# Exponentials over two PSUM banks, with root, turned tokens and logits rearranged, in an attention and mixture-of-experts kernel

## The chip, the cores and the metric
One core of a Trainium2 chip runs the whole program. A core has TensorE (matrix products, with separate weight loads), VectorE, ScalarE, GpSimd (called POOL) and SyncE (SP, whose queue issues most DMAs). They run side by side and wait for one another by semaphores. The metric is the device time of one execution, in microseconds (us).

## The reference
A block on 8 sequences of 1024 tokens with 256 features, in float32:

```python
x = x + attention(layernorm(x))      # 16 heads of 16, softmax(q k^T / 4) v, rotary turn on the last 256 tokens
x = x + ffn(layernorm(x))
# ffn: scores = softmax(h @ gate_w.T); each of 16 experts takes its top 128 tokens of a sequence,
#      eo = (gelu(x_tok @ Wg.T) * (x_tok @ Wu.T)) @ Wd.T * score, added back to its tokens;
#      a shared expert of the same shape (256 -> 512 -> 256) runs on all tokens.
# layernorm: (x - mean) / sqrt(var + 1e-5)
```
The input has 8 x 1024 rows.

## The kernel before, in words
Three stages follow each other: attention, the shared expert, the 16 experts.

**Attention.** The work of a sequence ("batch" b) is 64 steps, S = 0 to 63, and V = 64 b + S counts over all 512. Eight steps are a unit: four heads and half the queries. In step V, TensorE computes for four heads a score tile of 128 keys x 512 queries with the keys on the partitions ("turned scores", L811, two before and two after the weighing), ScalarE takes the exponential of each (L646), and two steps later (LAG) TensorE multiplies them with the values (`weigh_values`, L822, "the weighing"), accumulating eight steps in one PSUM bank `pv`. The softmax needs each query's maximum before that, so 12 steps ahead (LEAD) TensorE computes the same scores with the queries on the partitions (L800) into a ring of three banks, and VectorE takes four maxima a step out of it (L515). POOL splits the maxima of a unit into three bfloat16 parts (`split_maxima`), and SP turns them into the query tiles by a DMA transpose (`turn_maxima`).

The order is written by hand. `ORDER` lists everything that passes through the four banks `rot`: the four exponentials ("ex", V, j), then the items that `beside(V)` gives. The table BESIDE places these at a step: q, k and v of the next sequence, "xt" (its transposed tokens), and of the sequence before "aot", "proj", "x2t" and the gate's logits "lg"; "ot" (a finished unit) comes in steps S % 8 == 3. `PLACE` gives an item's number n: it uses bank n % 4. TensorE fills a bank when ScalarE has emptied item n - 4:

```python
        pe.wait_ge(rot_done, n - ROT + 1)          # L729
```
All engines keep their own program order. TensorE's in a step is: score rows m, m+1 (each waits for its ring bank, L798), turned scores 0 and 1, the weighing of V-2, score rows m+2, m+3, turned scores 2 and 3, the items beside. ScalarE's is: exponentials 0 to 3, in steps V % 8 == 1 the copy of `pv` (`evacuate`, L696) after exponential 2, then the items. The first weighing of the next unit, in a step S % 8 == 2, waits for that copy (L819).

VectorE takes four maxima a step, and in some steps joins the maxima of a unit (L521), takes reciprocals (L527), layernorm statistics (`gather_stats`, S = 0 to 3 and 21 to 24; `merge_stats`), and 1/sqrt(var + eps) by an integer trick and three Newton steps (`newton`, `rsqrt_step`, L36 to L50, S = 7 to 12 and 26 to 31, one operation at a time between maxima). POOL applies the layernorm (`normalise`, S = 13 to 16 and 33 to 36). "x2t" copies leave the second layernorm's transposed tokens in `XT`, which the next sequence's "aot" overwrites. `shift_logits` and `finish_gates` are the gate's softmax.

**Shared expert.** 16 chunks of 512 tokens. TensorE turns a chunk's tokens (`turn_tokens`, L1296, eight transposes) between products of the chunk before; ScalarE and VectorE split them into a high and a low part; `up` and `down` are the products in three passes (`three`, L61 to L63). The tokens come from the DRAM tensor `xn2` that attention has stored (`store_xn2`).

**Experts.** 32 chunks of 512 gathered rows run through the same function, with transposes of their own, and their results are added by indirect DMAs.

Of the kernel before, what the change touches and what calls it, by code (L numbers as in the profile page):

```python
# [65 lines left out]
def attention(nc, d, ident, SC, B):  # L66
# [36 lines left out]
    def beside(V):  # L103
# [7 lines left out]
        if S in table:  # L111
# [9 lines left out]
            + [("proj", B - 1, i) for i in range(TT)] + [("x2t", B - 1, h, half) for half in range(2) for h in range(KH)]  # L121
            + [("lg", B - 1, half) for half in range(2)])

# [15 lines left out]
    with ctx:  # L139
# [43 lines left out]
        nt1 = sb("nt1", [P, TT], F32)  # L183
        nt2 = sb("nt2", [P, TT], F32)
        shifted = sb("shifted", [P, TT, E], F32)
        powers = sb("powers", [P, TT, E], F32)
# [6 lines left out]
        ring = [ctx.enter_context(nc.psum_tensor(f"ring{i}", [P, 512], F32)) for i in range(RING)]  # L193
        rot = [ctx.enter_context(nc.psum_tensor(f"rot{i}", [P, 512], F32)) for i in range(ROT)]
        pv_bank = ctx.enter_context(nc.psum_tensor("pv", [P, 512], F32))
# [6 lines left out]
        x1_out = sem("x1_out")  # L202
        xn2_out = sem("xn2_out")
        wh_ready = sem("wh_ready")
        wl_ready = sem("wl_ready")
# [3 lines left out]
        bo_ready = sem("bo_ready")  # L209
        rstd_ready = [sem(f"rstd_ready{n}") for n in range(2)]  # L210
        xn_ready = [sem(f"xn_ready{h}") for h in range(2)]
        xn2_ready = [sem(f"xn2_ready{h}") for h in range(2)]
# [27 lines left out]
        def _(sp):  # L240
# [24 lines left out]
            def store_xn2(b):  # L265
                for h in range(2):
                    sp.wait_ge(xn2_ready[h], 2 * (b + 1))
                sp.dma_start(rows("xn2", b), XN2[:]).then_inc(xn2_out, 16)

            def turn_heads(b, g):  # L270

                sp.wait_ge(rope_done, 2 * ROPE_TILES * (b + 1))
                sp.wait_ge(q_biased, TT * (b + 1))
                sp.wait_ge(rot_done, done(("k", b, 5)))
                if b:
                    sp.wait_ge(rot_full, done(("ex", STEPS * (b - 1) + 16 * g + 15, 3)))
# [17 lines left out]
            for b in range(B):  # L294
# [22 lines left out]
                if b < B - 1:  # L317
                    turn_maxima(n + 8)
            store_x1(B - 1)
            store_xn2(B - 1)  # L320
            sp.wait_ge(x1_out, 16 * B)
            sp.wait_ge(xn2_out, 16 * B)

        @block.gpsimd
        def _(pool):
            own = Tally(pool_own)
            for n in range(2):
# [69 lines left out]
            def add_bias(b, n):  # L397
# [3 lines left out]
                nc.gpsimd.tensor_tensor(x, x, b_o[:].unsqueeze(1).to_broadcast([P, 2, H]), ALU.add).then_inc(bias_ready, 1)  # L401

            def normalise(n, b, out, src, ready, quarter):

                pool.wait_ge(rstd_ready[n], b)
                i = slice(2 * quarter, 2 * quarter + 2)
                shape = [P, 2, H]
                own.inc(nc.gpsimd.tensor_tensor(out[:, i, :], src[:, i, :], mv[n][:, i, 0:1].to_broadcast(shape),
                                                ALU.subtract))
                own.wait(pool)  # L410
                nc.gpsimd.tensor_tensor(out[:, i, :], out[:, i, :], rstd[n][:, i].unsqueeze(2).to_broadcast(shape),
                                        ALU.mult).then_inc(ready[quarter // 2], 1)
# [24 lines left out]
            for V in range(LAST):  # L437
# [15 lines left out]
                if more and b and S == 10:  # L453
                    clear_maxima(b + 1)
                if more and 13 <= S <= 16:
                    normalise(0, b + 2, XA, XA, xn_ready, S - 13)
# [9 lines left out]
        def _(dve):  # L466
# [10 lines left out]

            def merge_stats(n, tiles):

                own.wait(dve)  # L480
                for i in tiles:
                    own.inc(nc.vector.bn_aggr(mv[n][:, i, :], stats[:, i, :]))

# [45 lines left out]
            def shift_logits(b):  # L529

                dve.wait_ge(rot_done, done(("lg", b, 1)))
                own.inc(nc.vector.reduce_max(top[:], LG[:], AX.X))
# [34 lines left out]
            for V in range(-LEAD, LAST):  # L567
# [6 lines left out]
                if V >= 13 and V % 8 == 5:  # L574
                    weighted((V - 13) // 8)
                if more and 7 <= S <= 12:
                    newton(0, 2 * (S - 7))
                if prev and 26 <= S <= 31:
                    newton(1, 2 * (S - 26))
                if m < CHECKS:  # L580
# [11 lines left out]
                if more and S in (4, 5):  # L592
                    merge_stats(0, range(4 * (S - 4), 4 * (S - 3)))
                if more and 7 <= S <= 12:
                    newton(0, 2 * (S - 7) + 1)
                if prev and 21 <= S <= 24:
                    dve.wait_ge(x1_ready, TT * (b - 1) + 2 * (S - 20))
                    gather_stats(XR, (2 * (S - 21), 2 * (S - 21) + 1))
                if prev and S == 25:
                    for h in range(2):  # L600
                        dve.wait_ge(xn2_ready[h], 2 * (b - 1))
                    merge_stats(1, range(TT))
                if prev and 26 <= S <= 31:
                    newton(1, 2 * (S - 26) + 1)
                if prev and S == 50:
                    shift_logits(b - 1)
                if prev and S == 53:
                    finish_gates(b - 1)
# [23 lines left out]
        def _(act):  # L632
# [3 lines left out]
            def empty(item):  # L636
# [5 lines left out]
                if kind == "ex":  # L642
                    _, V, j = item
                    if j == 0 and V >= P_STEPS:
                        act.wait_ge(pv_done, V - P_STEPS + 1)
                    out = nc.scalar.activation(PR[V % P_STEPS][:, j, :], R[:], ACT.Exp, scale=0.25)  # L646
                elif kind in ("xt", "aot", "x2t"):
                    _, b, h, half = item
                    if kind == "xt" and b >= 2:
                        act.wait_ge(as_ready, 4 * (b - 1))  # L650
# [35 lines left out]
                elif kind == "lg":  # L686
                    _, b, half = item
                    if b:
                        act.wait_ge(shifted_ready, b)
                    out = nc.scalar.copy(LG[:, 4 * half:4 * half + 4, :], R[:, 0:4 * E].rearrange("p (t e) -> p t e", e=E))  # L690
                out.then_inc(rot_done, 1)

            def evacuate(unit):
# [28 lines left out]
        def _(pe):  # L722
# [15 lines left out]
            def fill(item):  # L738
# [38 lines left out]
                elif kind == "lg":  # L777
                    _, b, half = item
# [77 lines left out]
def feed_forward(nc, d, ident, SC, WT, IX, W, WH, WL, shared_out, B, shared):  # L856
# [20 lines left out]
    with ctx:  # L877
# [5 lines left out]

        XG = [sb(f"XG{c}", [P, CT, D], F32) for c in range(2)]
        XH = [sb(f"XH{c}", [P, KD, N], FR) for c in range(2)]
# [87 lines left out]
        def _(sp):  # L973
            if shared:
# [126 lines left out]
        def _(act):  # L1101
# [54 lines left out]
        def _(dve):  # L1156
# [131 lines left out]
        def _(pe):  # L1288
# [46 lines left out]

            turn_tokens(0, 0)
            if shared:
# [4 lines left out]
            def group(r, first, last):  # L1342
                for k in range(K):
# [20 lines left out]

def program(nc, d, B):
    with ExitStack() as ctx:
        SC = ctx.enter_context(nc.sbuf_tensor("gate_scores", [P, 1024 // P, B * E], F32))
# [40 lines left out]
```

## Time and profile before
| what | value |
|---|---|
| time, median of 3 runs | 2406.83 us (2402.03 to 2407.79) |
| the profiled execution's own time | 2401.16 us |
| its span | 2399.3 us |
| busy share: PE, DVE, ACT, POOL | 92%, 78%, 65%, 37% |
| granted TensorE clock, mean | 0.976 |

The busy share of each engine over the span in 40 slices of 60 us (9 is 90% or more) shows the stages: attention to slice 25, the shared expert to about slice 30, then the experts.

```profile
PE   4899999999999999999999987899997999999996
DVE  4999999999999999999999994566663554555553
ACT  2499888898888898898898886333332343434332
POOL 4051362451451451542542230000004666666664
```
A row of the page is one group of instructions: line, engine, operation, output and input tiles, count, then the busy time and the mean duration in ns. A busy TensorE is not one at its peak, since matrix products overlap.

### The profile page before, as it was taken

The page shows a single profiled execution, that of the slowest core. Times are in us where ns is not written, and L with a number is a line of the kernel's source. Part 1 is how long each engine was busy: PE and PEld are TensorE (multiplying, and loading weights), DVE is VectorE, ACT ScalarE, POOL GpSimd, SP SyncE. Part 2 cuts the span into 40 slices and gives each one's busy share as a digit, 9 for nine tenths or more (in the row PEclk, how much of TensorE's full clock was granted, in tenths as well). Part 3 has the DMA queues.
Part 4 walks back from the last instruction along what each step waited for, and adds up shares of the span by engine and source line. Part 5 has one row for each costly group of instructions (what it writes and reads, how often), then busy time and mean ns, then how long its engine had stood idle before and what let it go on. Part 6 is the DMA issues. An engine that isn't in the chain of part 4 may idle for free. (4 is left out here: it accounts for less than half of the span.)

```text
span 2399.3 us, 42479 instructions
## 1 busy us (share of the span) xinstructions
PE 2218.2 (92%) x15630; PEld 1288.6 (54%) x15630; DVE 1883.3 (78%) x3505; ACT 1561.1 (65%) x3040; POOL 895.3 (37%) x1287
## 2 busy tenths in 40 slices
PE   4899999999999999999999987899997999999996
PEld 3233333333333333333343323788886888888886
DVE  4999999999999999999999994566663554555553
ACT  2499888898888898898898886333332343434332
POOL 4051362451451451542542230000004666666664
PEclk8799999999999999999999999899998999999998
DMA  4002013012022121111112111323223455454543
GB/s 112 5 25 34 17 41 69 17 48 62 16 62 50 29 63 34 34 58 34 34 43 32 34 43 38 132 87 97 79 71 104 90 112 115 87 111 109 108 94 36
DMA packets 206756, 147.81 MB, mean 62 GB/s; under 512 B 109952, under 2 KB 193792, under 8 KB 206592
## 3 DMA queue, kind: packets, MB, share of 16 engines
q1 hardware_dynamic: 182016, 112.08, 17.3%
q0 software_dynamic: 24576, 33.57, 8.1%
q8 instruction: 100, 1.64, 0.3%
q14 instruction: 64, 0.52, 0.1%
HBM read 78.50 MB, written 41.94 MB: 50 GB/s over the span
## 5 line engine op out<-in xcount | busy, mean ns | idle before, releaser
L515 DVE TENSOR_REDUCE sb_MX<-ring 128x1 f32<-128x512 f32 x2048 | 1281.9, 680 | 67.7 <-PE ring L800 51.5
L646 ACT ACTIVATE sb_PR<-rot 128x512 f32<-128x512 f32 x2048 | 1119.5, 608 | 145.7 <-PE rot L811 130.2
L800 PE MATMUL ring<-sb_KT,sb_QT 32*128 32x512 bf16 x2048 | 526.6, 391 | 92.3 <-DVE sb_MX L515 76.9
L822 PE MATMUL pv<-sb_PR,sb_VA 128*32 128x512 f32 x4096 | 546.5, 606 | 2.6 <-ACT sb_OT L696 0.6
L800 PEld LDWEIGHTS ring<-sb_KT,sb_QT 32*128 32x128 bf16 x2048 | 129.9, 91 | 707.4 <-DVE sb_MX L515 649.0
L811 PE MATMUL rot<-sb_QT,sb_KT 32*128 32x512 bf16 x2048 | 405.1, 386 | 0.9
L1113 ACT ACTIVATE ex_GL<-ex_gu 128x512 f32<-128x512 f32 x128 | 76.5, 597 | 348.6 <-PE ex_gu L63 346.4
L1180 DVE TENSOR_TENSOR ex_HF<-ex_GL,ex_gu 128x512 f32<-128x512 f32 x128 | 87.4, 682 | 252.0 <-ACT ex_GL L1113 252.0
L1077 POOL DMA_INDIRECT out<-ex_YS,ex_rows_out x128 | 208.9, 1632 | 44.1 <-issue 43.7
L1034 POOL TENSOR_TENSOR ex_pool_scratch<-identity 128x1 f32<-128x1 f32 x96 | 35.1, 366 | 472.4 <-POOLq L877 325.8
L61 PE MATMUL ex_gu<-ex_XH,weights_high 128*128 128x512 f32 x512 | 201.1, 393 | 2.4 <-DVE ex_XL L1172 2.4
L62 PE MATMUL ex_gu<-ex_XL,weights_high 128*128 128x512 f32 x512 | 200.7, 392 | 0.0
L63 PE MATMUL ex_gu<-ex_XH,weights_low 128*128 128x512 f32 x512 | 200.5, 392 | 0.0
L364 POOL CAST sb_QP<-sb_MX 128x16 bf16<-128x16 f32 x64 | 16.3, 255 | 421.2 <-DVE sb_MX L521 421.2
L1113 ACT ACTIVATE sh_GL<-sh_gu 128x512 f32<-128x512 f32 x64 | 38.2, 597 | 175.9 <-PE sh_gu L63 175.9
L61 PE MATMUL ex_y<-weights_high,ex_HH 128*128 128x256 f32 x512 | 148.2, 289 | 2.9 <-DVE ex_HL L1184 2.9
L822 PEld LDWEIGHTS pv<-sb_PR,sb_VA 128*32 128x32 f32 x4096 | 80.9, 108 | 123.2 <-issue 65.2
L63 PE MATMUL ex_y<-weights_high,ex_HL 128*128 128x256 f32 x512 | 145.7, 285 | 0.0
L62 PE MATMUL ex_y<-weights_low,ex_HH 128*128 128x256 f32 x512 | 145.7, 285 | 0.0
L61 PE MATMUL rot<-sb_WH,sb_XH 128*128 128x256 f32 x384 | 129.5, 337 | 14.6 <-ACT sb_PR L646 5.7
L1055 POOL DMA_INDIRECT ex_XG<-xn,ex_rows_in x128 | 125.7, 982 | 40.3 <-issue 39.6
L1180 DVE TENSOR_TENSOR sh_HF<-sh_GL,sh_gu 128x512 f32<-128x512 f32 x64 | 43.6, 682 | 103.3 <-ACT sh_GL L1113 103.2
(158 smaller groups left out, 4042.8 us busy)
## 6 DMA issues: line engine op xcount, KB each, us to landing
sb_XA<-x SPq DMA_DIRECT2D x8, 1024.0 KB, 5.7
sb_XR<-x SPq DMA_DIRECT2D x8, 1024.0 KB, 5.7
out<-sb_XR SPq DMA_DIRECT2D x8, 1024.0 KB, 4.6
xn<-sb_XN SPq DMA_DIRECT2D x8, 1024.0 KB, 4.4
sh_XG<-xn SPq DMA_DIRECT2D x16, 512.0 KB, 5.9
sh_X<-out SPq DMA_DIRECT2D x16, 512.0 KB, 5.2
weights<-WgT SPq DMA_DIRECT2D x16, 512.0 KB, 4.0
weights<-WuT SPq DMA_DIRECT2D x16, 512.0 KB, 6.4
```

Source lines behind the costliest of these rows:

```text
L61: nc.tensor.matmul(out, a_hi, b_hi, start=first, stop=False)
L62: nc.tensor.matmul(out, a_hi, b_lo, start=False, stop=False)
L63: return nc.tensor.matmul(out, a_lo, b_hi, start=False, stop=last)
L515: nc.vector.reduce_max(MX[:, unit % 2, half, j, qt % 4:qt % 4 + 1], ring[m % RING][:], AX.X).then_inc(ring_done, 1)
L646: out = nc.scalar.activation(PR[V % P_STEPS][:, j, :], R[:], ACT.Exp, scale=0.25)
L800: nc.tensor.matmul(ring[m % RING][:], QT[g][r, P * qt:P * qt + P], KT[g][r, 512 * half:512 * half + 512], start=True, stop=True, tile_posi ...
L811: nc.tensor.matmul(R[:], KT[g][r, P * kt:P * kt + P], QT[g][r, 512 * qh:512 * qh + 512], start=True, stop=True, tile_position=(r.start, 0) ...
L822: out = nc.tensor.matmul(pv_bank[head(j), :], VA[b % 2][:, kt, 4 * g + j, :], PR[V % P_STEPS][:, j, :], start=(kt == 0), stop=(kt == TT - 1))
L1055: nc.gpsimd.indirect_dma_start(out=XG[k % 2][:, t, :], out_offset=None, in_=d["xn2"], in_offset=bass.IndirectOffsetOnAxis(ap=rows_in[:, b: ...
L1077: nc.gpsimd.indirect_dma_start(out=d["out"], out_offset=bass.IndirectOffsetOnAxis(ap=rows_out[:, b:b + 1], axis=0), in_=YS[k % 2][:, t, :] ...
L1113: nc.scalar.activation(GL[f % 2][:], gu[f % 2][:, 0, 0:N], ACT.Gelu).then_inc(gelu_ready, 1)
L1180: nc.vector.tensor_tensor(HF[f % 2][:], GL[f % 2][:], gu[f % 2][:, 1, 0:N], ALU.mult).then_inc(hf_ready, 1)
```

## The change
- **Exponentials.** The four `rot` banks become one tensor. A new function takes the exponential of banks n and n+1 in one instruction of 128 x 1024 and releases both at its end, except where n % 4 == 3 (the two don't lie next to each other). The copy of `pv` stands after exponential 3.
- **Root.** `newton` leaves VectorE's loop. At S = 7 and 27 POOL computes (var + eps) to the power of -0.5 and one Newton step, six operations on 128 x 8. The first and the last sequence's roots outside the loop stay on VectorE.
- **Turned tokens.** SP stores `XT` to a DRAM tensor `xn2T` late in each batch; ScalarE's first "aot" copy waits for that. The shared expert loads its chunks from `xn2T` and has no transposes; ScalarE and VectorE split them straight from `XG`.
- **Logits.** "lg" comes in four items of two token tiles (S = 47 to 50) in place of two items of four (S = 47, 48); the gate's steps move two steps later.

```diff
--- before.py
+++ after.py
...
-              43: (1, "k", 4), 44: (1, "q", 5), 45: (1, "k", 5), 47: (-1, "lg", 0), 48: (-1, "lg", 1),
+              43: (1, "k", 4), 44: (1, "q", 5), 45: (1, "k", 5), 47: (-1, "lg", 0), 48: (-1, "lg", 1), 49: (-1, "lg", 2),
+              50: (-1, "lg", 3),
...
-        rot = [ctx.enter_context(nc.psum_tensor(f"rot{i}", [P, 512], F32)) for i in range(ROT)]
+        rots = ctx.enter_context(nc.psum_tensor("rot", [P, ROT, 512], F32))
+        rot = [rots[:, i, :] for i in range(ROT)]
...
+            def store_turned(b):
+                sp.wait_ge(rot_done, done(("x2t", b, KH - 1, 1)))
+                sp.dma_start(d["xn2T"][bass.ds(b * H, H), :].rearrange("(k p) t -> p k t", p=P), XT[:]).then_inc(xt2_out, 16)
...
+                if b:
+                    store_turned(b - 1)
...
+            def inverse_root(n, count):
+
+                y = rstd[n]
+                pool.wait_ge(mv_ready[n], count)
+                own.inc(nc.gpsimd.tensor_scalar(spread[:], mv[n][:, :, 1], EPS, None, ALU.add))
+                own.wait(pool)
+                own.inc(nc.gpsimd.tensor_tensor(y[:], spread[:], minus_half[:], ALU.pow))
+                own.wait(pool)
+                own.inc(nc.gpsimd.tensor_tensor(refine[:], y[:], y[:], ALU.mult))
+                own.wait(pool)
+                own.inc(nc.gpsimd.tensor_tensor(refine[:], refine[:], spread[:], ALU.mult))
+                own.wait(pool)
+                own.inc(nc.gpsimd.tensor_scalar(refine[:], refine[:], -0.5, 1.5, ALU.mult, ALU.add))
+                own.wait(pool)
+                nc.gpsimd.tensor_tensor(y[:], y[:], refine[:], ALU.mult).then_inc(rstd_ready[n], 1)
...
+                if more and S == 7:
+                    inverse_root(0, b + 1)
+                if b and S == 27:
+                    inverse_root(1, b)
...
-                if more and 7 <= S <= 12:
-                    newton(0, 2 * (S - 7))
-                if prev and 26 <= S <= 31:
-                    newton(1, 2 * (S - 26))
...
+                    merge_stats(0, range(4 * (S - 4), 4 * (S - 3)), S == 5)
...
-                if prev and S == 50:
+                    merge_stats(1, range(TT), True)
+                if prev and S == 52:
                     shift_logits(b - 1)
-                if prev and S == 53:
+                if prev and S == 55:
...
-                    if j == 0 and V >= P_STEPS:
-                        act.wait_ge(pv_done, V - P_STEPS + 1)
                     out = nc.scalar.activation(PR[V % P_STEPS][:, j, :], R[:], ACT.Exp, scale=0.25)
                 elif kind in ("xt", "aot", "x2t"):
                     _, b, h, half = item
+                    if kind == "aot" and b and h == 0 and half == 0:
+                        act.wait_ge(xt2_out, 16 * b)
...
+            def exponentials(V, j):
+
+                n = PLACE[("ex", V, j)]
+                if j == 0 and V >= P_STEPS:
+                    act.wait_ge(pv_done, V - P_STEPS + 1)
+                if n % ROT == ROT - 1:
+                    empty(("ex", V, j))
+                    empty(("ex", V, j + 1))
+                else:
+                    act.wait_ge(rot_full, n + 2)
+                    nc.scalar.activation(PR[V % P_STEPS][:, j:j + 2, :], rots[:, n % ROT:n % ROT + 2, :], ACT.Exp,
+                                         scale=0.25).then_inc(rot_done, 2)
...
-                    for j in range(4):
-                        empty(("ex", V, j))
-                        if j == 2 and V >= 9 and V % 8 == 1:
-                            evacuate((V - 9) // 8)
+                    exponentials(V, 0)
+                    exponentials(V, 2)
+                    if V >= 9 and V % 8 == 1:
+                        evacuate((V - 9) // 8)
                 for item in beside(V):
                     empty(item)
-                if V >= STEPS and V % STEPS == 51:
+                if V >= STEPS and V % STEPS == 53:
...
-                    pe.wait_ge(rot_done, done(("x2t", b, 1, half)))
-                    for m in range(4):
-                        i = 4 * half + m
+                    _, b, n = item
+                    pe.wait_ge(rot_done, done(("x2t", b, 1, n // 2)))
+                    for m in range(2):
+                        i = 2 * n + m
...
-                        sp.wait_ge(turned_full, n - 1)
-                    sp.dma_start(XG[k % 2][:], rows("xn2", n)).then_inc(x_in[k % 2], 16)
+                        sp.wait_ge(xl_ready, n - 1)
+                    sp.dma_start(XG[k % 2][:], d["xn2T"][bass.ds(r * D, D), N * k:N * k + N].rearrange("(k p) t -> p k t", p=P)
+                                 ).then_inc(x_in[k % 2], 16)
...
-                act.wait_ge(turned_full, n + 1)
-                nc.scalar.copy(XH[k % 2][:], turned[:, :, 0:N]).then_inc(xh_ready, 1)
+                if shared:
+                    act.wait_ge(x_in[k % 2], 16 * (r + 1))
+                    if not (isinstance(n, int) and n < 2):
+                        act.wait_ge(gu_full, KF * (n - 1))
+                    nc.scalar.copy(XH[k % 2][:], XG[k % 2][:]).then_inc(xh_ready, 1)
+                else:
+                    act.wait_ge(turned_full, n + 1)
+                    nc.scalar.copy(XH[k % 2][:], turned[:, :, 0:N]).then_inc(xh_ready, 1)
...
-                nc.vector.tensor_tensor(XL[k % 2][:], turned[:, :, 0:N], XH[k % 2][:].bitcast(F32),
-                                        ALU.subtract).then_inc(xl_ready, 1)
+                nc.vector.tensor_tensor(XL[k % 2][:], XG[k % 2][:] if shared else turned[:, :, 0:N],
+                                        XH[k % 2][:].bitcast(F32), ALU.subtract).then_inc(xl_ready, 1)
...
-                    if not (last and k == K - 1):
+                    if not shared and not (last and k == K - 1):
```

## Rows read from the trace of the kernel before
**Rows 1.** Busy times by stretch: stretch and length, then each engine's busy us.
```profile
core 0: us, PE busy (x) PEld busy (x) DVE busy (x) ACT busy (x) POOL busy (x), PEclk, DMA share, GB/s
607.00:782.80 175.80, 165.62 (x1334) 64.46 (x1336) 171.06 (x337) 155.96 (x319) 70.77 (x117) 1.00 0.18 43
1500.00:1785.00 285.00, 275.76 (x1611) 244.58 (x1611) 174.32 (x284) 87.85 (x145) 0.00 (x0) 0.97 0.30 96
```
**Rows 2.** Waits from 240 to 1320 us: who <- whom, total us, times, longest.
```profile
PEld ring L800 <- DVE sb_MX L515: 474.9, 734, 1.2
...
DVE sb_MX L515 <- PE ring L800: 14.4, 24, 0.9
```
**Rows 3.** Timeline of a plain step: start us, length us, engine, line, tiles, count.
```profile
713.14 0.39 PE L800 MATMUL ring<-sb_KT,sb_QT 32*128 32x512 bf16 x2
...
714.32 0.38 PE L800 MATMUL ring<-sb_KT,sb_QT 32*128 32x512 bf16 x1 [0.31 <-DVE sb_MX L515]
...
714.64 1.07 PE L822 MATMUL pv<-sb_PR,sb_VA 128*32 128x512 f32 x8
715.64 0.39 PE L800 MATMUL ring<-sb_KT,sb_QT 32*128 32x512 bf16 x2
```
**Rows 4.** Timeline across steps 41 and 42 of the same batch.
```profile
720.78 0.39 PE L811 MATMUL rot<-sb_QT,sb_KT 32*128 32x512 bf16 x2
...
721.26 0.60 ACT L646 ACTIVATE sb_PR<-rot 128x512 f32<-128x512 f32 x1 [0.21 <-PE rot L811]
...
721.76 0.58 ACT L696 COPY sb_OT<-pv 128x512 f32<-128x512 f32 x1
721.95 0.39 PE L811 MATMUL rot<-sb_QT,sb_KT 32*128 32x512 bf16 x2
...
722.39 1.06 PE L822 MATMUL pv<-sb_PR,sb_VA 128*32 128x512 f32 x8
```
**Rows 5.** Timeline at the next step's turned score 1.
```profile
723.66 1.14 ACT L646 ACTIVATE sb_PR<-rot 128x512 f32<-128x512 f32 x2
...
724.85 0.09 PEld L811 LDWEIGHTS rot<-sb_QT,sb_KT 32*128 32x128 bf16 x1 [0.20 <-ACT sb_PR L646]
```
**Rows 6.** Line 1109 by form: ns least/median/most, first and last start.
```profile
L1109 ACT CAST sh_XH<-sh_turned x16: 1006/1018/1021, 1511.4 to 1762.1; 128x1024 fp32r<-128x1024 f32 x16
```
**Rows 7.** Timeline of VectorE among the root's operations.
```profile
681.58 0.16 DVE L40 TENSOR_SCALAR sb_nt<-sb_mv 128x8 f32<-128x8 f32 x1
681.65 1.28 DVE L515 TENSOR_REDUCE sb_MX<-ring 128x1 f32<-128x512 f32 x2
```
**Rows 8.** Timeline in step 8 of the same batch.
```profile
631.06 1.27 POOL L381 TENSOR_TENSOR sb_AL<-sb_XT,sb_AH 128x512 fp32r<-128x512 f32 x1
...
631.22 1.13 DVE L45 TENSOR_SCALAR sb_rstd<-sb_rstd 128x8 int32<-128x8 int32 x1
```
**Rows 9.** Timeline at the first logits item.
```profile
737.04 1.96 PE L783 MATMUL rot<-sb_gw,sb_XT 128*128 128x16 f32 x16
...
739.35 0.69 DVE L515 TENSOR_REDUCE sb_MX<-ring 128x1 f32<-128x512 f32 x1 [0.93 <-PE ring L800]
```
**Rows 10.** Timeline of a chunk of the shared stage.
```profile
1550.43 1.03 PE L1296 MATMUL sh_turned<-identity,sh_XG 128*128 128x128 f32 x8
...
1551.22 0.36 PE L61 MATMUL sh_y<-weights_high,sh_HH 128*128 128x256 f32 x1
```
**Rows 11.** Timeline of SP, end of the batch.
```profile
774.20 1.19 SPq L285 DMA_TRANSPOSE sb_QT<-sb_QP  x1
```
**Rows 12.** Timeline of ScalarE, first "aot" copy of the next batch.
```profile
785.21 0.59 ACT L655 COPY sb_XT<-rot 128x512 f32<-128x512 f32 x1
```
**Rows 13.** DMA issues of the page: KB each, median us to landing.
```profile
xn<-sb_XN SPq DMA_DIRECT2D x8, 1024.0 KB, 4.4
```
**Rows 14.** Timelines of VectorE and POOL around the first layernorm.
```profile
624.74 0.37 DVE L482 BATCH_NORM_AGGREGATE sb_mv<-sb_stats 128x2 f32<-128x6 f32 x4
...
647.60 1.04 POOL L408 TENSOR_TENSOR sb_XA<-sb_XA,sb_mv 128x512 f32<-128x512 f32 x1
```

More of the change, by code:

```diff
@@ L121, in attention @@
             + [("proj", B - 1, i) for i in range(TT)] + [("x2t", B - 1, h, half) for half in range(2) for h in range(KH)]
-            + [("lg", B - 1, half) for half in range(2)])
+            + [("lg", B - 1, n) for n in range(4)])
     ORDER = HEAD + [item for V in range(-LEAD, LAST)
@@ L184, in attention @@
         nt2 = sb("nt2", [P, TT], F32)
+        minus_half = sb("minus_half", [P, TT], F32)
+        spread = sb("spread", [P, TT], F32)
+        refine = sb("refine", [P, TT], F32)
         shifted = sb("shifted", [P, TT, E], F32)
@@ L203, in attention @@
         xn2_out = sem("xn2_out")
+        xt2_out = sem("xt2_out")
         wh_ready = sem("wh_ready")
@@ L210, in attention @@
         rstd_ready = [sem(f"rstd_ready{n}") for n in range(2)]
+        mv_ready = [sem(f"mv_ready{n}") for n in range(2)]
         xn_ready = [sem(f"xn_ready{h}") for h in range(2)]
@@ L318, in _ @@
                     turn_maxima(n + 8)
+                if b:
+                    store_turned(b - 1)
             store_x1(B - 1)
             store_xn2(B - 1)
+            store_turned(B - 1)
+            sp.wait_ge(xt2_out, 16 * B)
             sp.wait_ge(x1_out, 16 * B)
@@ L326, in _ @@
             own = Tally(pool_own)
+            own.inc(nc.gpsimd.memset(minus_half[:], -0.5))
             for n in range(2):
@@ L476, in gather_stats, with merge_stats @@
                     own.inc(nc.vector.bn_stats(stats[:, i, :], src[:, i, :]))
-            def merge_stats(n, tiles):
+            def merge_stats(n, tiles, last=False):
                 own.wait(dve)
                 for i in tiles:
-                    own.inc(nc.vector.bn_aggr(mv[n][:, i, :], stats[:, i, :]))
+                    step = nc.vector.bn_aggr(mv[n][:, i, :], stats[:, i, :])
+                    if last and i == tiles[-1]:
+                        step.then_inc(mv_ready[n], 1)
+                    else:
+                        own.inc(step)
             def newton(n, k):
@@ L529, in shift_logits @@
             def shift_logits(b):
-                dve.wait_ge(rot_done, done(("lg", b, 1)))
+                dve.wait_ge(rot_done, done(("lg", b, 3)))
                 own.inc(nc.vector.reduce_max(top[:], LG[:], AX.X))
@@ L592, in _ @@
                 if more and S in (4, 5):
-                    merge_stats(0, range(4 * (S - 4), 4 * (S - 3)))
-                if more and 7 <= S <= 12:
-                    newton(0, 2 * (S - 7) + 1)
+                    merge_stats(0, range(4 * (S - 4), 4 * (S - 3)), S == 5)
                 if prev and 21 <= S <= 24:
@@ L601, in _ @@
                         dve.wait_ge(xn2_ready[h], 2 * (b - 1))
-                    merge_stats(1, range(TT))
-                if prev and 26 <= S <= 31:
-                    newton(1, 2 * (S - 26) + 1)
-                if prev and S == 50:
+                    merge_stats(1, range(TT), True)
+                if prev and S == 52:
                     shift_logits(b - 1)
-                if prev and S == 53:
+                if prev and S == 55:
                     finish_gates(b - 1)
@@ L686, in empty @@
                 elif kind == "lg":
-                    _, b, half = item
+                    _, b, n = item
                     if b:
                         act.wait_ge(shifted_ready, b)
-                    out = nc.scalar.copy(LG[:, 4 * half:4 * half + 4, :], R[:, 0:4 * E].rearrange("p (t e) -> p t e", e=E))
+                    out = nc.scalar.copy(LG[:, 2 * n:2 * n + 2, :], R[:, 0:2 * E].rearrange("p (t e) -> p t e", e=E))
                 out.then_inc(rot_done, 1)
+            def exponentials(V, j):
[9 more added lines that the diff above has]
+                                         scale=0.25).then_inc(rot_done, 2)
             def evacuate(unit):
@@ L777, in fill @@
                 elif kind == "lg":
-                    _, b, half = item
-                    pe.wait_ge(rot_done, done(("x2t", b, 1, half)))
-                    for m in range(4):
-                        i = 4 * half + m
+                    _, b, n = item
+                    pe.wait_ge(rot_done, done(("x2t", b, 1, n // 2)))
+                    for m in range(2):
+                        i = 2 * n + m
                         for h in range(KH):
@@ L882, in sem @@
             return ctx.enter_context(nc.semaphore(tag + name))
-        XG = [sb(f"XG{c}", [P, CT, D], F32) for c in range(2)]
+        XG = [sb(f"XG{c}", [P, KD, N] if shared else [P, CT, D], F32) for c in range(2)]
         XH = [sb(f"XH{c}", [P, KD, N], FR) for c in range(2)]
@@ L1107, in split_tokens @@
                 n = r * K + k
-                act.wait_ge(turned_full, n + 1)
-                nc.scalar.copy(XH[k % 2][:], turned[:, :, 0:N]).then_inc(xh_ready, 1)
+                if shared:
[3 more added lines that the diff above has]
+                    nc.scalar.copy(XH[k % 2][:], XG[k % 2][:]).then_inc(xh_ready, 1)
+                else:
+                    act.wait_ge(turned_full, n + 1)
+                    nc.scalar.copy(XH[k % 2][:], turned[:, :, 0:N]).then_inc(xh_ready, 1)
             def gelu(n, f):
@@ L1334, in down @@
                 out.then_inc(y_full, 1)
-            turn_tokens(0, 0)
+            if not shared:
+                turn_tokens(0, 0)
             if shared:
@@ L1365, in program @@
 def program(nc, d, B):
+    d["xn2T"] = nc.dram_tensor("xn2T", (B * D, 1024), F32, kind="Internal").ap()
     with ExitStack() as ctx:
```

## The prediction
> **What bounds the kernel now.** I read the busy times by stretch first. A batch inside the attention stage takes 175.8 us (six alike), with VectorE busy 171.1, TensorE 165.6, ScalarE 156.0; in the shared-expert stage TensorE is busy 275.8 of 285 us, VectorE 174.3 [rows 1]. So attention looks VectorE-bound and the shared stage is TensorE-bound. The list of waits then shows that TensorE's weight loads stood 474.9 us (of 1080) until a maximum had emptied a ring bank, and VectorE only 14.4 us for TensorE [rows 2]. I went to the timeline because three engines near 90% in one loop need not be bound by throughput. A plain step V (four maxima, four turned scores, no item beside) takes 715.64 - 713.14 = 2.49 us. Four maxima at 0.60 us start to start would be 2.40. The 2.49 is a circle through the three ring banks: score row at 714.32 after a maximum freed its bank, weighing at 714.64, next rows at 715.64 (end .39 later), next maximum [rows 3]. The weighing (1.07 us) stands in TensorE's queue behind the turned scores 0 and 1 of its step, so whatever holds turned score 1 holds the rows, and then VectorE. That is the place to look at for the pairs.
>
> **The pairs (exponentials).** Banks are handed out in turn, four of them. 791 of the 1024 pairs become one instruction; the 233 whose first bank is the fourth stay two. ScalarE's time of one: a 128x1024 copy out of two banks took 1.018 us [rows 6] where one bank's exponential took 0.60 [rows 4]. Two single ones end 0.49 + 0.60 = 1.09 us after the first began. So a pair ends a little earlier (0.07), but its first bank comes free 0.42 later. The price lies between 1.02 and 2 x 0.60 = 1.20; I take 1.02, the row for the same size and the same two banks. The Trainium skill ("ScalarE: Activation LUTs", What ACT_TABLE_LOAD costs) puts an ACTIVATE at 186 ns + 0.833 N: an estimate of 1.04 for 1024, which the 1.018 row supports.
>
> Who waits for that first bank? With no item beside step V, turned score 1 of V+1 takes the bank of exponential 1 of V, long free. With one item beside (a projection, q, k, v, a transpose), it is shifted by one and takes that of exponential 2 of V, the first of the second pair. That this bank can hold TensorE is in the trace once: exponential 2 ended at 723.66 + 1.14 = 724.80, and turned score 1's weights loaded at 724.85, idle before it until ScalarE [rows 5]. Normally it just fits: turned scores 2 and 3 of a step end at 721.17, ScalarE begins at 721.26, ends 721.86, turned score 1 of the next step goes at 721.95 [rows 4]. As a pair it ends at 721.26 + 1.02 = 722.28, plus the 0.05 of rows 5: 722.33, 0.38 late. The same subtraction in the other steps gives 0.26 to 0.39, mostly 0.33, and the queue hands it on unshortened, since ring, maximum and next exponential all move with it.
>
> Counting from the order of items: in a full batch some 29 steps have one item beside and a joined second pair. About 7 of them lie where VectorE is the later one anyhow (statistics in steps 0 to 5 and 21 to 25, the gate's work), and five coincide with the next paragraph. That leaves 16 at 0.32 = 5.1 us a batch.
>
> **The evacuation behind the pair.** In steps 1 mod 8, ScalarE copied the output bank between exponentials 2 and 3 (721.76, 0.58 us), and the weighing of the next step started on its end, 722.39 [rows 4]. Now it stands behind both: 721.26 + 1.02 less the 0.10 of overlap, + 0.58 + 0.05 = 722.81, 0.42 late. Where the pair is split, two exponentials stand ahead and it is about the same. Eight a batch, two of them hidden by statistics: 6 x 0.42 = 2.5 us.
>
> Loss per full batch 7.6 us, six of them 46; batches 0 and 7, which have fewer items, about 6.8 each: **59 us**. In the last 12 steps, without maxima, ScalarE is the bound, and 24 pairs at 0.07 give back at most 1.6; I take 1. With a pair of 1.20 us instead, 22 late steps x 8 x 0.18 add 30.
>
> **Inverse root to POOL.** VectorE loses 13 small instructions in each of 14 places. They do not cost their 0.16 us: one starts at 681.58, the next maximum at 681.65, the two maxima take 1.20, so 1.27 a pair against 1.245 in a plain step [rows 7, 3]; comparing whole stretches of steps, 0.4 us a batch. But one of them took 1.13 us instead of 0.16, at 631.22, while POOL ran a subtraction with two inputs from 631.06 to 632.33 [rows 8]; that recurs in six batches and saves 1.0 each. Together 1.4 x 7 = **10 us** less. The power on POOL is in no row; its neighbours there run 0.2 to 1.3 us, six of them under 8 us. Cover: means are ready at 625.1, POOL first uses the root at 647.60 [rows 14]. So 0, and up to 1 us a batch if it held the split maxima.
>
> **Logits in four quarters.** Sixteen products (1.96 us) keep the next score rows back until 738.93, and VectorE stood 0.93 before its next maximum [rows 9]; two such steps a batch, the two gaps 2.0 us together against a plain step. Eight products are 0.89 shorter, which leaves about 0.1 each, four times; what the late banks cost in those steps is in the count above. 1.9 x 7 = **13 us** less.
>
> **Turned tokens stored.** In the shared stage eight transposes took 1551.22 - 1550.43 = 0.79 us of a TensorE that never waits [rows 10]. 15 chunks x 0.79 = **12 us** less; the first chunk waits for weights anyway. ScalarE and VectorE have far under the chunk's 17.5 us of work, so TensorE stays the bound. The price is 1 MB more to store per batch and a wait in ScalarE's queue ahead of "aot", with all exponentials behind it. SP can issue the store after the transpose at 774.20 + 1.19; ScalarE's first aot copy is at 785.21 [rows 11, 12]. Such a store lands in 4.4 us [rows 13]: covered by 5 us. At the end of attention the store follows the gate's work within a microsecond: 0 to 1.
>
> **Sum**: 59 - 1 - 10 - 13 - 12 = +23, with +1 for the end: +24 on the profiled execution's 2401.2 (span 2399.3) = 2425. The median of the runs shown is 5.7 us above that execution; I forecast midway for the same change, 2429.
>
> **The rivals.**
> (a) *The banks are free in time.* ScalarE idles 20 us a batch and joining shortens its work, so nothing is late and the gains stand: 2407 - 36 = 2371. The Trainium skill ("Perfetto Trace Analysis", Optimizing Scalar/DVE Operations) says grouping helps "if the engine is saturated"; ScalarE at 156 of 176 us is not. Its section Matmuls wants groups to rotate through the banks so that emptying overlaps the next group, which pairs make coarser. Against (a): rows 5. 0.12.
> (b) *Only the evacuation is late*: the late turned scores are taken up by slack that I don't see. 8 x 2.5 = 20 against 35: 2407 - 16 = 2391. For it: every late step leaves VectorE ahead. Against: in a plain step the circle, not VectorE, is the later. 0.12.
> (c) *The first pair too.* The item beside needs exponential 0's bank; in rows 4's step it has some 0.09 us to spare after joining. If a pair takes 0.1 more than the copy, that margin is gone and all 22 places grow: 8 x 22 x 0.1 = 18, 2447. It outweighs the forecast from 1.07 us a pair. 0.14.
> Forecast 0.62. Forecast and (c) are slower than before, (a) and (b) faster; a measurement here can tell about 0.3% (7 us). From the forecast's lower edge and (b)'s upper some fall within that. Faster 0.20, same 0.07, slower 0.73. The likeliest case's own range is 2414 to 2442; to leave two in ten out it must reach towards (b) and (c): 2395 to 2448.
>
> **What would show it.** A full batch (now 175.8) should take 175.8 + 7.6 - 3.3 = 180.1 us; the shared chunk 16.75 instead of 17.54. A pair should take 1.02 us; turned scores should show waits for ScalarE of some 0.3 us in steps after an item, weighings in steps 2 mod 8 should start on the copy's end, and VectorE's waits for the ring should rise from 14 to over 40 us in the same six batches. ScalarE's busy time should fall. I am wrong if batches stay under 175 us (then (a) or (b)), if VectorE waits elsewhere, or if ScalarE's aot copy stands waiting for the store.

## The result: 2456 us against 2406 before

The changed kernel took 2456.22 us (median of four runs, 2451.39 to 2458.73), the kernel before 2405.57 in the same job (2402.03 to 2407.79). The ratio is 1.021, with a 95% interval of 1.0187 to 1.0232: slower, clear of noise and as forecast, but by 51 us and not by 24, and 8 us above the range. Whether it is more than 2% slower the interval leaves open. The profiled execution took 2458.73 us, the longest of the four; the one of the kernel before (2401.16) was shorter than all four of its runs here. From the page of the changed kernel, the span, the busy times and the costliest groups:

```profile
span 2456.8 us, 41793 instructions
PE 2259.9 (92%) x15502; PEld 1286.9 (52%) x15502; DVE 1878.5 (76%) x3323; ACT 1530.8 (62%) x2265; POOL 932.5 (38%) x1372
...
L555 DVE TENSOR_REDUCE sb_MX<-ring 128x1 f32<-128x512 f32 x2048 | 1286.0, 683 | 136.7 <-PE ring L845 125.6
L735 ACT ACTIVATE sb_PR<-rot 128x1024 f32<-128x1024 f32 x791 | 811.8, 1027 | 210.0 <-PE rot L856 192.8
...
L676 ACT ACTIVATE sb_PR<-rot 128x512 f32<-128x512 f32 x466 | 253.8, 599 | 42.9 <-PE rot L856 36.6
```

The pairs are there, 791 of them, at 1027 ns each on average. ScalarE's busy time fell from 1561.1 to 1530.8 us, and the kernel became slower. The next rows answer to [rows 1]: the same full batch and the shared stage of the changed kernel (length, then busy time of each engine, granted clock, DMA).

```profile
631.80:815.30 183.50, 172.09 (x1331) 65.47 (x1328) 170.13 (x310) 152.09 (x223) 76.10 (x129) 1.00 0.19 47
1584.40:1858.90 274.50, 270.64 (x1532) 239.25 (x1533) 180.01 (x293) 88.99 (x147) 0.00 (x0) 0.98 0.28 90
```

The batch is 7.7 us longer than the 175.8 of before, though VectorE and ScalarE are busy for less of it, and TensorE's matmuls are as many (1331, before 1334). The waits from 240 to 1320 us answer to [rows 2]:

```profile
PEld ring L845 <- DVE sb_MX L555: 415.3, 609, 1.1
...
DVE sb_MX L555 <- PE ring L845: 68.3, 173, 0.7
...
PEld rot L856 <- ACT sb_PR L735: 52.8, 164, 0.6
...
PEld pv L867 <- ACT sb_OT L741: 23.7, 47, 0.9
```

VectorE's wait for the ring went from 14.4 to 68.3 us. Turned scores now wait for a pair of exponentials 164 times, 0.32 us on average; in the kernel before they waited for an exponential 12 times, 2.3 us in all. The weighing's wait for the copy of the output bank (last line) was 15.4 us, 49 times, before. The table says where the 57.5 us between the two profiled spans arose. "Last maximum" is the start of the last one:

| stretch | before | after | change |
|---|---|---|---|
| start to last maximum | 1448.0 | 1511.5 | +63.5 |
| last maximum to the shared stage's first product | 66.0 | 73.0 | +7.0 |
| shared stage | 286.6 | 274.5 | -12.1 |
| the rest, expert stage | 598.7 | 597.9 | -0.8 |

The late turned score, in the timeline of the changed kernel (start, length, engine, line, tiles). It answers to [rows 4] and to [rows 5]:

```profile
670.90 0.39 PE L856 MATMUL rot<-sb_QT,sb_KT 32*128 32x512 bf16 x2
...
671.47 1.03 ACT L735 ACTIVATE sb_PR<-rot 128x1024 f32<-128x1024 f32 x1 [0.69 <-PE rot L856]
...
672.12 0.39 PE L845 MATMUL ring<-sb_KT,sb_QT 32*128 32x512 bf16 x2
...
672.55 0.09 PEld L856 LDWEIGHTS rot<-sb_QT,sb_KT 32*128 32x128 bf16 x1 [0.34 <-ACT sb_PR L735]
```

Scores 2 and 3 ended at 671.29. The pair began 0.18 later, ended at 672.50, and 0.05 after that turned score 1 of the next step went, at 672.55. Turned score 0, which needs another bank, had gone with the ring rows at 672.13; in [rows 4] the two went together. So this step lost 0.42 us. The place of the output bank's copy:

```profile
752.12 1.02 ACT L735 ACTIVATE sb_PR<-rot 128x1024 f32<-128x1024 f32 x1 [0.37 <-PE rot L856]
...
753.04 0.58 ACT L741 COPY sb_OT<-pv 128x512 f32<-128x512 f32 x1
...
753.67 0.16 PEld L867 LDWEIGHTS pv<-sb_PR,sb_VA 128*32 128x32 f32 x8 [0.39 <-ACT sb_OT L741]
```

From the pair's start to the weighing it is 1.55 us now; in [rows 4] it was 722.39 - 721.26 = 1.13.

### The profile page after: what moved, and what is told of

Read it like the earlier page. It is cut to its first block and busy times, and to the rows that moved or that the text cites. A ratio compares the mean times of both kernels' runs of the same rounds, so it can differ in the third digit from the quotient of the medians.

```text
span 2456.8 us, 41793 instructions
## 1 busy us (share of the span) xinstructions
PE 2259.9 (92%) x15502; PEld 1286.9 (52%) x15502; DVE 1878.5 (76%) x3323; ACT 1530.8 (62%) x2265; POOL 932.5 (38%) x1372
## 5 line engine op out<-in xcount | busy, mean ns | idle before, releaser
L735 ACT ACTIVATE sb_PR<-rot 128x1024 f32<-128x1024 f32 x791 | 811.8, 1027 | 210.0 <-PE rot L856 192.8
L845 PE MATMUL ring<-sb_KT,sb_QT 32*128 32x512 bf16 x2048 | 499.2, 392 | 81.7 <-DVE sb_MX L555 68.2
L856 PE MATMUL rot<-sb_QT,sb_KT 32*128 32x512 bf16 x2048 | 473.4, 387 | 9.8 <-ACT sb_PR L735 3.0
L845 PEld LDWEIGHTS ring<-sb_KT,sb_QT 32*128 32x128 bf16 x2048 | 121.1, 91 | 676.6 <-DVE sb_MX L555 606.3
L676 ACT ACTIVATE sb_PR<-rot 128x512 f32<-128x512 f32 x466 | 253.8, 599 | 42.9 <-PE rot L856 36.6
L856 PEld LDWEIGHTS rot<-sb_QT,sb_KT 32*128 32x128 bf16 x2048 | 114.8, 91 | 82.1 <-ACT sb_PR L735 75.0
```

Of the source, the lines that this page charges most:

```text
L735: nc.scalar.activation(PR[V % P_STEPS][:, j:j + 2, :], rots[:, n % ROT:n % ROT + 2, :], ACT.Exp, scale=0.25).then_inc(rot_done, 2)
L845: nc.tensor.matmul(ring[m % RING][:], QT[g][r, P * qt:P * qt + P], KT[g][r, 512 * half:512 * half + 512], start=True, stop=True, tile_posi ...
L856: nc.tensor.matmul(R[:], KT[g][r, P * kt:P * kt + P], QT[g][r, 512 * qh:512 * qh + 512], start=True, stop=True, tile_position=(r.start, 0) ...
```

## The experiments

The theory before them: the whole loss comes from the pairs, by late turned scores, by late copies and by something that the forecast had not counted; the three other edits gain what they were said to. The rival is a lower granted clock, or one of the other edits. All ratios are to the kernel before on the same chip. Where two changed kernels are compared, they can come from different jobs; the kernel before had medians of 2402.51 to 2406.50 us in the four jobs.

**The pairs alone.** The kernel before with only this:

```diff
+            def exponentials(V, j):
+                n = PLACE[("ex", V, j)]
...
+                if n % ROT == ROT - 1:
+                    empty(("ex", V, j))
+                    empty(("ex", V, j + 1))
+                else:
+                    act.wait_ge(rot_full, n + 2)
+                    nc.scalar.activation(PR[V % P_STEPS][:, j:j + 2, :], rots[:, n % ROT:n % ROT + 2, :], ...).then_inc(rot_done, 2)
```

> Only the exponentials of two banks and the copy of the output bank behind them; root, tokens and logits as before. Theory A (the pairs hold the bank and the copy, each late place 0.42 us instead of the 0.33 that was forecast, because a pair also starts 0.19 us after its score where a single one starts 0.10): about 22 late places x 0.43 x 8 = +75 us, some less where the old root and logits work covers a few, so +60 to +80 over the kernel before, a full batch about 185. Theory B (the pairs cost the forecast +59 and the rest of the miss is in the other three edits, which brought less than 35): +55 to +60, a full batch 183.4.

2489.22 us, 1.0349 (1.033 to 1.0369): 83 us more than before, 3 above the top of what I had said. The full batches took 185.9 to 187.4 us, 186.6 on average.

**All but the pairs.** The changed kernel with

```diff
-                    exponentials(V, 0)
-                    exponentials(V, 2)
-                    if V >= 9 and V % 8 == 1:
-                        evacuate((V - 9) // 8)
+                    for j in range(4):
+                        empty(("ex", V, j))
+                        if j == 2 and V >= 9 and V % 8 == 1:
+                            evacuate((V - 9) // 8)
```

> The changed kernel with four single exponentials and the copy in its old place; root, tokens and logits as changed. Theory A: the forecast gains stand, -35 us (2371), a full batch 172.5. Theory B: the three edits together bring clearly less, -10 to -20 us, a full batch over 173.5.

2367.69 us, 0.9848 (0.9832 to 0.9865), the fastest kernel of all, 38 us below before. Its full batch and VectorE's wait for the ring:

```profile
601.00:773.60 172.60, 164.36 (x1332) 63.96 (x1328) 169.06 (x311) 156.47 (x323) 76.04 (x129) 1.00 0.20 50
```
```profile
DVE sb_MX L555 <- PE ring L847: 3.2, 12, 0.3
```

The batch differs from the changed kernel's by 10.9 us, VectorE's busy time in it by only 1.1 and TensorE's by 7.7. VectorE's wait is 3.2 against 68.3, which is 11 us for each of the 5.9 batches between 240 and 1320 us. The loss of the pairs is 88.5 us by the medians (2456.22 - 2367.69).

**The root alone** (the kernel before with only `inverse_root` on POOL in place of the Newton steps):

```diff
-                if more and 7 <= S <= 12:
-                    newton(0, 2 * (S - 7))
...
+                if more and S == 7:
+                    inverse_root(0, b + 1)
```

> Only the inverse root on POOL. Theory A and the forecast: -10 us (1.4 a full batch). Theory B: 0 to -5, since without the pairs VectorE is held by the circle through the ring and small operations cost it nothing; the batch shortens by the 1.0 us of the one long shift alone or not at all.

2396.20 us, 0.9959 (0.9946 to 0.9972): 10 us less; a full batch 174.2, 1.6 less where 1.4 was said.

**The logits alone** (four items of two tiles each):

```diff
-                    for m in range(4):
-                        i = 4 * half + m
+                    for m in range(2):
+                        i = 2 * n + m
```

> Only the logits in four items. Both theories expect the two gaps of 1.0 us in VectorE's maxima to shrink to four of 0.1: -13 us (1.9 a full batch). If the four items hold TensorE as long as two did, 0.

2394.51 us, 0.9952 (0.9935 to 0.9968): 12 us less; a full batch 174.1, 1.6 less where 1.9 was said.

**Which pairs.** In the changed kernel a pair is joined only where a test allows it. Split the second pair where exactly one item stands beside the step:

```diff
-                if n % ROT == ROT - 1:
+                if n % ROT == ROT - 1 or not (j == 0 or len(beside(V)) != 1):
```

> The changed kernel, but the second pair of a step is joined only where not exactly one item follows (the copy stays behind exponential 3). Theory A (bank of exponential 2 held for turned score 1): 16 places x 0.43 x 8 = 55 us go, 2456 becomes about 2400. Theory C (joining costs something at every pair, wherever it stands): only the share of pairs that are split comes back, about 29 of 103 a batch of 88 us, 2431.

2398.69 us, 0.9965 (0.9953 to 0.9978): 57.5 us of the loss gone, nearly two thirds.

Split the second pair of steps 1 mod 8 and copy between its halves:

```diff
-                if n % ROT == ROT - 1:
+                if n % ROT == ROT - 1 or not (j == 0 or not (V >= 9 and V % 8 == 1)):
                     empty(("ex", V, j))
+                    if j == 2 and V >= 9 and V % 8 == 1:
+                        evacuate((V - 9) // 8)
                     empty(("ex", V, j + 1))
```

> The changed kernel, but in steps 1 mod 8 exponentials 2 and 3 are single and the copy of the output bank stands between them as before. Theory A: 6 places x 0.5 x 8 = 24 us go, about 2432. Theory C: 8 of 103 pairs a batch, 7 us, 2449.

2431.87 us, 1.0103 (1.0087 to 1.012): 24 us of the loss gone.

Both together:

```diff
+                if n % ROT == ROT - 1 or not (j == 0 or (len(beside(V)) != 1 and not (V >= 9 and V % 8 == 1))):
```

> Both: second pairs joined only where neither one item nor the copy follows; all first pairs joined as in the changed kernel. Theory A: the whole 88 us between the changed kernel and the one with four single exponentials go, 2366 to 2375. Theory C: about 66 us of them stay with the joined pairs less the split ones, over 2400.

2379.50 us, 0.9885 (0.9868 to 0.9901): 77 us gone, and 12 left against the kernel without pairs. I had expected 2366 to 2375. What is left joined here is every first pair, and the second pairs that hold nobody by the count. So these are not free: 12 / 8 = 1.5 us a batch. The run doesn't tell the first pairs from the second.

**The wait for two scores, without a pair.** The kernel without pairs, its exponentials 0 and 2 waiting until both scores of their pair are there:

```diff
                     for j in range(4):
+                        if j % 2 == 0:
+                            act.wait_ge(rot_full, PLACE[("ex", V, j)] + 2)
                         empty(("ex", V, j))
```

> The three other edits with four single exponentials, of which 0 and 2 wait for both scores of their pair before they start, as the joined one has to. It tells the wait from the size. If the later start of a joined exponential (0.19 us after its score, a single one 0.10) is the wait for the second score, singles start at 0.19 too and the time rises by 16 x 8 x 0.06 = 8 us over 2368; if it belongs to the instruction over two banks, they start at 0.13 or less and the time is 2368 to 2371.

2378.74 us, 0.9886 (0.9869 to 0.9902): 11 us more than without the wait. In the profiled executions 8.4 us of it lie before the last maximum, where 8 had been said, and 3 behind it. Over all steps from 240 to 1320 us in which ScalarE stood idle before it, an exponential began (median) 0.094 us after the last score ended in the kernel without pairs, 0.154 in this one, and 0.180 in the changed kernel (0.188 for its pairs alone). Two thirds of the later start come with waiting for the second score, with single instructions over one bank; the rest comes with the pair.

**The copy late, without a pair** (the kernel without pairs, the copy behind exponential 3):

```diff
-                        if j == 2 and V >= 9 and V % 8 == 1:
+                        if j == 3 and V >= 9 and V % 8 == 1:
```

> The three other edits with four single exponentials and the copy of the output bank behind exponential 3 instead of between 2 and 3. Nothing is joined. Theory A: the copy ends 0.49 us later (the distance of two singles), seven places a batch feel 0.4 to 0.5 of it: +24 us over 2368, 2392. If the copy's place mattered only together with a joined exponential, 2368 to 2372.

2393.03 us, 0.9956 (0.9939 to 0.9972): 25 us more than with the copy between, as in the changed kernel (24). The waits show the same two entries grow, from 15.2 and 3.2 us:

```profile
PEld pv L869 <- ACT sb_OT L741: 39.6, 50, 0.8
...
DVE sb_MX L555 <- PE ring L847: 23.9, 44, 0.6
```

**The bank held, without a pair.** Single exponentials that begin as early as before, but exponential 3 releases its own bank and that of exponential 2:

```diff
-                out.then_inc(rot_done, 1)
+                if kind != "ex" or item[2] < 2:
+                    out.then_inc(rot_done, 1)
+                elif item[2] == 3:
+                    out.then_inc(rot_done, 2)
```

> The three other edits with four single exponentials; exponential 2 does not release its bank, exponential 3 releases both at its end. Nothing is joined, no start is later. Theory A: the bank comes free 0.49 us later, less the 0.09 of margin, in 28 places a batch (also where the changed kernel splits the pair): 28 x 0.4 x 7.5 = +84 us at most, and not under +50 for the 16 places it shares with the changed kernel: 2420 to 2450. If what costs is the joined instruction itself, 2368 to 2375.

2476.09 us, 1.0296 (1.0276 to 1.0316), 108 us over the kernel without pairs, more than I had said (up to 2450), and more than the pairs themselves:

```profile
DVE sb_MX L555 <- PE ring L850: 85.3, 196, 1.0
PEld rot L861 <- ACT sb_PR L676: 84.3, 229, 0.9
```

It holds the bank in every step, the 233 pairs that the changed kernel splits among them, and where the copy stands between the two exponentials it holds it for the copy as well. It shows the sign and the mechanism without any wider instruction: turned scores wait 229 times, against 164 with the pairs. Its size isn't that of the change.

**Joining only in the last steps** (there are no maxima there; this kernel ran once):

```diff
+                if n % ROT == ROT - 1 or not (V >= 500 and not (j == 2 and V % 8 == 1)):
```

> The three other edits, with exponentials joined only in the last 12 steps, where there are no maxima and ScalarE was taken as the bound. The forecast's part for that stretch: 24.8 us from the last maximum to the last exponential become 23.8. If the weighing between the scores is what paces these steps, or the release in pairs holds TensorE there too, 24.8 to 27.

From the end of the last maximum to the end of the last exponential it took 25.15 us, against 25.01 without pairs: joining gave nothing back. (From start to start it is 24.81 against 25.03, but the last start is then that of a pair, which stands where the third of the four exponentials would.) In all 2370.11 us by the single run, no gain over 2367.69.

## Why the forecast had the sign and missed the size

**The step that failed: the price of a held bank.** The mechanism was right and its size was not. The forecast gave the pairs 59 us up to the last maximum. The spans show 85.6 there (changed kernel less the one without pairs: 74.8 up to the end of batch 6, 10.8 in batch 7). A full batch lost 10.9 on average, against 7.6 said. Here is the batch of the windows above, taken apart in both traces from the start of each step's last turned score to that of the next step's:

- 17 steps with one item beside and a joined second pair lost 0.33 to 0.48 each, mostly 0.42, and 6.9 in all (one lost 0.70, of which 0.29 came back two steps later). The forecast had 16 such steps at 0.32, 5.1 in all. Its price held the pair's duration, 1.02, but took [rows 4]'s start of a single exponential (721.26, 0.09 after the scores' end) for the pair's. A pair started 0.18 after its scores. Of these 0.09, 0.06 is the wait for the second score, which the run with the wait alone shows; the other 0.03 wasn't isolated.
- Seven places of the copy lost 0.25 to 0.52 each, 3.3 in all. The forecast had six at 0.42, 2.5 in all. It took two places as hidden by statistics: the one in steps 1 and 2 was (0.03), the one in steps 25 and 26 lost 0.25. The run with the copy between gave 24 us back, 3 a batch.
- The other steps lost 0.7 together. The forecast gave nothing for pairs that hold nobody. The run that spares both late places still loses 1.5 a batch to them, and the wait alone, with no pair, costs 0.9 a batch.

So 6.9 + 3.3 + 0.7 = 10.9 took the place of 5.1 + 2.5 + 0 = 7.6.

**Rival (c), in half.** It had said that 0.09 us of margin stands between the first pair and the item beside, and that a pair longer by 0.1 would take it: 2447. The pair wasn't longer. It began later by that same 0.09, which for a bank is one and the same. Its sum grew only the 22 late places and left out what the other pairs lose, so that it too fell short. Rivals (a) and (b) are out: turned scores wait 164 times, and splitting their pairs gives back more than twice what the copy does.

**The last steps and the stage change.** The forecast had joining give 1 us back in the last steps. Of their 24 pairs only 16 are joined, and joining alone gave nothing. Instead the stretch from the last maximum to the shared stage's first product grew by 7.0 us. From the end of the last maximum to the end of the last exponential the changed kernel took 27.28 us, the one before 24.81; the rest lies behind it. In this stretch the granted clock is 0.50, the lower of its two levels (1.2 GHz), for longer. TensorE was busy 5.9 of the 10.2 us before the clock first fell there in the kernel before (at 1489.9), and 3.8 of the 6.9 before it fell for the longest time in the changed one (at 1556.2). Windows of the kernel before, then of the changed one:

```profile
1500.10:1517.20 17.10, 7.86 (x30) 6.73 (x30) 7.21 (x10) 5.75 (x7) 0.00 (x0) 0.50 0.59 197
```
```profile
1556.00:1590.10 34.10, 17.80 (x69) 16.23 (x70) 13.29 (x42) 8.74 (x15) 0.00 (x0) 0.50 0.61 209
1440.00:1446.80 6.80, 6.45 (x32) 1.26 (x24) 4.54 (x9) 3.59 (x6) 2.71 (x6) 0.51 0.00 0
```

The last row lies inside batch 7, before the last maximum. Over the steps around it the changed kernel fell 2.7 us further behind the one without pairs, where the same steps of other batches lose 0.3. So some 2.4 of the 10.8 us of batch 7 go with the clock. TensorE had stood 0.52 us for the late copy just before; whether that brought the clock down isn't shown.

Read microsecond by microsecond, the half clock lasts some 24 us in all between the last maximum and that product's first chunk in the kernel before, 27 in the kernel without pairs, 31 with both places spared, 34 with the wait for both alone, 37 with the root alone, and 41 both with the pairs before an item split and in the changed kernel. The stretch from the last maximum took 66.0, 66.6, 68.9, 69.6, 70.9, 72.0 and 73.0 us in the same order. So 17 us more at half clock go with 7 us more. The pairing isn't exact: with the logits alone 27 us go with 69.6.

The edits need not have made this difference. The kernel before, run eleven times on one chip, took 2401.73 to 2405.90 us in the five executions with a mean granted clock of 0.975 to 0.977, and 2406.18 to 2408.26 in the six with 0.973. Seventeen us at half clock in 2400 are 0.0035 of the mean, which is about that distance. The profiled execution of the kernel before had 0.976 and that of the changed kernel 0.972; a run of the changed kernel with 0.976 took 2451.39. The root alone and the wait alone have no pair and sit in the middle of the row. So most of the 7 us can be which execution was profiled; what moves the clock is open.

**What was right.** The three other edits: 35 us said, 34.2 between the profiled spans (38 by the medians). The root 10 said and 10 measured; the logits 13 and 12; the shared chunk 16.75 said, 16.66 measured. The new store is covered. SP issues it, and ScalarE's first "aot" copy goes ten microseconds later without waiting; from the page, the store lands in 4.2:

```profile
807.60 0.58 SPq L279 DMA_DIRECT2D xn2T<-sb_XT  x1
```
```profile
817.88 0.58 ACT L687 COPY sb_XT<-rot 128x512 f32<-128x512 f32 x1
```
```profile
xn2T<-sb_XT SPq DMA_DIRECT2D x8, 1024.0 KB, 4.2
```

The root on POOL, which no row had priced, has its power in one long instruction and is done by 660.66, in step 7 of a batch; the first layernorm takes it in step 13:

```profile
657.87 1.67 POOL L425 TENSOR_TENSOR sb_rstd<-sb_spread,sb_minus_half 128x8 f32<-128x8 f32 x1
...
660.46 0.20 POOL L433 TENSOR_TENSOR sb_rstd<-sb_rstd,sb_refine 128x8 f32<-128x8 f32 x1
```

The duration of a pair: 1.02 said from the copy of the same size, 1.027 on the page. The Trainium skill ("ScalarE: Activation LUTs", What ACT_TABLE_LOAD costs) gives an estimate of 1.04 by 186 ns + 0.833 N; the trace agrees within 0.02. The Trainium skill's page "Perfetto Trace Analysis" (Optimizing Scalar/DVE Operations) ties grouping to a saturated engine. ScalarE is busy 156.5 of the 172.6 us of a batch without pairs, and joining took 4.4 us of work off it and added 10.9 to the batch. The page's condition was not met, and joining did not help here.

**Sum of the miss.** On the profiled executions the forecast was +24 and the outcome +57.5. Of the 33.5 between them, 26.6 come from the pairs up to the last maximum (20 in the six full batches, 2.6 in batch 0 and before it, 4 in batch 7, of which 2.4 at half clock), and 7.4 from the last steps and the stage change (73.0 - 66.6 = 6.4, and the 1 that joining didn't give back). The rest nearly cancels: the other edits brought 34.2 for 35, and no run priced the 1 us said for the store at the end. By the medians the kernel before and 24 make 2429.6, and 2456.22 is 26.6 above that, about the part up to the last maximum alone. So the medians need nothing from the stage change.

## What to carry to other kernels

Joining two instructions over two banks saves the fixed cost of one of them, but it moves two events: the first bank comes free at the end of both, and the work begins only when both inputs are there. Price these two events against the margin of each one who waits, place by place, and take the start of an instruction that waits for two producers from a row with such a wait, not from a single one. Here a saving of 4.4 us of ScalarE's work a batch cost 10.9 us, and leaving the pairs out gave the fastest kernel, 2367.69 us; joining only where nobody waits (2379.50) did not beat it.

## What the chip showed that was not expected

An exponential that waits for the second of two scores begins 0.154 us after it ends, one that waits for its own alone 0.094. The two scores end 0.004 us apart (median), so the 0.06 comes though no data is later by as much. The power of 128x8 values took 1.67 us on POOL where its neighbours of the same size took 0.20 to 0.24. And the kernel before, run eleven times without any edit, took 2401.7 to 2405.9 us with a mean granted clock of 0.975 or more and 2406.2 to 2408.3 with 0.973. In single profiled executions of seven kernels the half-speed stretch at the change of stages lasted from 24 us in all to 41, and 17 us more of it went with about 7 us more. A difference of a few us between two profiled spans is to be read with the clock rows beside it.
